# Quantising the fp4 stage's weights during the fourth rotary layer's feed-forward, and two tile copies taken ahead of the magnitudes

## The reference

```python
def fp4_quant_dequant(x):               # along the last dimension
    xb = x.reshape(shape[:-1] + (shape[-1] // 16, 16))
    scale = jnp.maximum(jnp.max(jnp.abs(xb), axis=-1, keepdims=True) / 6.0, 1e-12)
    xn = xb / scale
    idx = jnp.searchsorted(_MID, jnp.abs(xn))     # midpoints of 0 .5 1 1.5 2 3 4 6
    return (_GRID[idx] * jnp.sign(xn) * scale).reshape(shape)
def fp4_linear(x, w):
    return jnp.einsum('bsk,nk->bsn', fp4_quant_dequant(x), fp4_quant_dequant(w))
h = _silu(fp4_linear(x, w_gate)) * fp4_linear(x, w_up)      # w_gate, w_up: (352, 128)
return fp4_linear(h, w_down)                                # w_down: (128, 352)
```

## Time and profile before

| | us |
|---|---|
| median of 3 runs (6010.93 to 6014.99) | 6013.17 |
| profiled execution, its own time | 6008.89 |
| its span, first to last instruction | 6007.2 |
| fp4 stage within the span, first instruction 5394.99 to its last, ending 5698.75 | 304 |
| fourth layer's feed-forward alone on TensorE, about 4422 to 4549 | 127 |

### The profile page before, as it was taken

One profiled execution on the slowest core, in us unless ns is written; L12 is line 12 of the kernel. 1 busy time (PEld: TensorE's weight loads), 2 busy tenths in 40 slices (PEclk: granted clock), 3 DMA queues, 4 the chain that ended last, 5 costly groups with the idle time before them and its releaser, 6 DMA issues. The chain is left out here.

```text
span 6007.2 us, 119421 instructions
## 1 busy us (share of the span) xinstructions
PE 5516.8 (92%) x37438; PEld 3426.2 (57%) x37453; DVE 4177.6 (70%) x9588; ACT 2809.3 (47%) x4608; POOL 2256.1 (38%) x3170
## 2 busy tenths in 40 slices
PE   7997999999999899999999999999997879886687
PEld 5664444444444477657775677567754456644564
DVE  6785666666666688658874788478846866578764
ACT  4554222222222355545555555555555655534354
POOL 6662000000001466436653666356623532153212
PEclk9998999999999899999999999999998999898899
DMA  4333333333333555325542555055510000000002
GB/s 134 107 105 103 97 96 95 98 97 96 97 97 100 142 159 156 87 79 158 156 127 59 141 159 158 27 150 157 157 33 5 0 7 0 1 4 0 2 0 64
DMA packets 526333, 527.07 MB, mean 88 GB/s; under 512 B 55698, under 2 KB 436705, under 8 KB 503780
## 3 DMA queue, kind: packets, MB, share of 16 engines
q1 hardware_dynamic: 517684, 517.90, 31.5%
q10 hardware_dynamic: 8320, 5.25, 0.4%
HBM read 337.88 MB, written 185.07 MB: 87 GB/s over the span
## 5 line engine op out<-in xcount | busy, mean ns | idle before, releaser
L1121 DVE TENSOR_REDUCE a_mx<-a_unit 128x2 f32<-128x512 f32 (+1 forms) x1536 | 1033.9, 688 | 309.1 <-PE a_unit L1412 303.6
L1261 ACT ACTIVATE a_prob<-a_slot 128x1536 f32<-128x1536 f32 x512 | 742.9, 1451 | 550.1 <-PE a_slot L1435 464.8
L2098 ACT ACTIVATE f_silu<-f_pG 128x512 f32<-128x512 f32 x528 | 314.7, 597 | 935.1 <-PE f_pG L2182 921.1
L1410 PE MATMUL a_unit<-a_sk,a_sq 96*128 96x128 bf16 (+1 forms) x4096 | 597.5, 249 | 42.4 <-DMA a_sk<-a_kscratch 26.7
L2033 DVE TENSOR_TENSOR f_gated<-f_spread,f_silu 128x512 f32<-128x512 f32 x512 | 362.9, 709 | 341.2 <-ACT f_silu L2098 296.6
L2150 PE MATMUL f_pO<-f_hidden,f_wd 128*128 128x512 f32 x1056 | 546.3, 599 | 14.1 <-DVE f_hidden L2035 13.5
L60 POOL TENSOR_SCALAR f_veps<-f_moments 128x4 f32<-128x4 f32 (+1 forms) x112 | 25.3, 226 | 1420.1 <-DVE f_moments L1909 1020.4
L2182 PE MATMUL f_pG<-f_xnT,f_wg 128*128 128x512 f32 x1056 | 541.6, 594 | 0.0
L2186 PE MATMUL f_pU<-f_xnT,f_wu 128*128 128x512 f32 x1056 | 540.7, 594 | 0.0
L1412 PE MATMUL a_unit<-a_maskq,identb 128*128 128x256 bf16 (+1 forms) x1536 | 481.7, 314 | 2.1 <-issue 2.1
L1063 POOL TENSOR_SCALAR_AFFINE_SELECT a_prob<-a_prob 128x512 f32<-128x512 f32 x384 | 244.5, 637 | 519.4 <-ACT a_prob L1261 506.1
(11 more groups left out here) (473 smaller groups left out, 12165.1 us busy)
## 6 DMA issues: line engine op xcount, KB each, us to landing
f_spread<-f_scratch SPq DMA_DIRECT2D x1024, 128.0 KB, 2.9
a_sq<-a_qscratch SPq DMA_DIRECT2D x128, 768.0 KB, 5.6
a_sk<-a_kscratch SPq DMA_DIRECT2D x160, 384.0 KB, 6.6
a_qscratch<-a_parts SPq DMA_DIRECT2D x288, 192.0 KB, 2.2
a_qscratch<-a_parts SPq DMA_DIRECT2D x288, 128.0 KB, 2.2
a_kscratch<-a_parts SPq DMA_DIRECT2D x160, 192.0 KB, 2.2
a_kscratch<-a_parts SPq DMA_DIRECT2D x160, 128.0 KB, 2.2
a_qscratch<-a_parts SPq DMA_DIRECT2D x288, 64.0 KB, 1.8
```

Source lines behind the costliest of these rows:

```text
L1121: v.tensor_reduce(dst, src, op=ALU.max, axis=AX.X, negate=True).then_inc(red_done, 1)
L1261: act.activation(prob[gr % 2][:, :], slot[:, :], ACT.Exp, scale=SCALE).then_inc(exp_done, 1)
L1410: pe.matmul(bank[:, at * wide:(at + 1) * wide], q, sk[b][0:KM, gr * GH + h, 0:wide], start=(at == 0), stop=False)
L2098: act.activation(silu[c % 2][:, :], pG[c % 2][:, :], ACT.Silu).then_inc(silu_done, 1)
```

## The change

1. A class `Fp4Weights` takes over what `weights()` did. It owns the turned weights and seven semaphores for the whole program. In the fourth rotary layer's feed-forward, SyncE loads the weights and GpSimd blanks the unused rows once the last attention output is added; VectorE scales at s = 4 and 5 and rounds at s = 7 and 8; ScalarE takes the magnitudes at s = 6 and copies turned tiles at s = 9, 10 and 11, behind the second gelu; TensorE turns them at s = 9, 10 and 11, behind `widen(s, 0)`. The work lies in tiles of the attention. The same code leaves the fp4 stage.
2. In the fp4 stage's `step`, ScalarE copies turned tiles 0 and 1 ahead of the magnitudes of the gated rows.
3. The feed-forward's output tile `oT` is the attention's `ctxp`; two unused functions and two small unused tiles go.

```diff
+    def on_vector(self, v, chain, s):
+        if s == 4:
+            v.wait_ge(self.w_in, 80)
+            v.wait_ge(self.blank, 2)
+            self.scale(v, chain, self.raw, self.nsc, self.y)
+        if s == 5:
+            self.scale(v, chain, self.rawd, self.nscd, self.yd)
+            v.sem_inc(self.scaled, 1)
+        if s == 7:
+            v.wait_ge(self.magnitudes, 1)
+            self.round_to(v, chain, self.y, self.mag, self.nsc, self.done)
+        if s == 8:
+            self.round_to(v, chain, self.yd, self.magd, self.nscd, self.magd)
+            v.sem_inc(self.rounded, 1)
+    def on_scalar(self, act, s):
+        if s == 6:
+            act.wait_ge(self.scaled, 1)
+            act.activation(self.mag, self.y, ACT.Abs, scale=self.TWO_BITS)
+            act.activation(self.magd, self.yd, ACT.Abs, scale=self.TWO_BITS).then_inc(self.magnitudes, 1)
+        if s in (9, 10):
+            act.wait_ge(self.turned, s - 8)
+            at = (s - 9) * self.I
+            act.activation(self.wgu[:, at:at + self.I], self.bank[:, 0:self.I], ACT.Copy).then_inc(self.taken, 1)
...
+    def on_tensor(self, pe, s, ident):
+        if s in (9, 10):
+            pe.wait_ge(self.rounded, 1)
+            if s == 10:
+                pe.wait_ge(self.taken, 1)
+            for j, (lo, cnt) in enumerate(self.CUTS):
+                at = (3 * (s - 9) + j) * D
+                ins = pe.transpose(self.bank[:, lo:lo + cnt], self.done[0:cnt, at:at + D], ident[0:cnt, 0:cnt])
+            ins.then_inc(self.turned, 1)
...
@@ rotary_layers, SyncE and GpSimd, behind the last main_steps
+                sp.wait_ge(op_taken, SEQS)
+                q.load(sp)
...
+                g.wait_ge(op_taken, SEQS)
+                q.fill(g)
                 feed(False)
@@ VectorE, end of step s of feed
                         feed_stats(s)
+                        if not following:
+                            v.drain()
+                            q.on_vector(v, chain, s)
@@ fp4_feed_forward, VectorE
-                    if isinstance(n, int) and n == -3:
-                        weights()
@@ fp4_feed_forward, ScalarE
                     gate(1)
+                    if is_block(n - 1):
+                        turned_hidden(n - 1, 0)
+                        turned_hidden(n - 1, 1)
                     if is_block(n):
                         act.wait_ge(yh_done, n + 1)
                         act.activation(absh[:, :], yh[b][:, :], ACT.Abs, scale=TWO_BITS).then_inc(ah_done, 1)
-                    if is_block(n - 1):
-                        turned_hidden(n - 1, 0)
                     if is_block(n + 2):
                         act.wait_ge(yx_done, n + 3)
                         act.activation(absx[:, :], yx[:, :], ACT.Abs, scale=TWO_BITS).then_inc(ax_done, 1)
                     if is_block(n - 1):
-                        turned_hidden(n - 1, 1)
                         turned_hidden(n - 1, 2)
```

More of the change, by code:

```diff
@@ L111, in later @@
     return not isinstance(n, int) or n >= least
[L114 to L154, removed]
 KPART = [0, 1, 2, 0, 1, 0]
@@ L962, in rotary_layers @@
         mrow_in = [k.sem(f"mrow_in{b}") for b in range(4)]
+        q = core["fp4"]
+        q.work(o.rest[:, :, :].rearrange("p c t -> p (c t)"), o.f32s[:, :, :].rearrange("p c t -> p (c t)"), prob[0], prob[1], cT, ring[1])
         (w_in, fstats_done, frstd_done, fxn_done, ft_pe, fxnT_done, h_pe, gelu_done, o_pe, o_done, r_pe, r_taken,
@@ L1327, in feed @@
                         gelu(s + 1, 1)
+                        if not following:
+                            q.on_scalar(act, s)
                         if following and s in EARLY and EARLY[s] > -5:
@@ L1564, in feed @@
                                 o.turn_rows(pe, EARLY[s])
+                            if c == 0 and not following:
+                                q.on_tensor(pe, s, ident)
                             if c == 2:
@@ L2785, in fp4_feed_forward @@
         with nc.Block() as block:
-            @block.sync
-            def _(sp):
-                for c, name in ((0, "wg"), (3, "wu")):
-                    sp.dma_start(raw[:, c:c + 2, :], w[name][0:2 * P, :].rearrange("(c p) d -> p c d", p=P)
-                                 ).then_inc(w_in, 16)
-                    sp.dma_start(raw[0:I - 2 * P, c + 2, :], w[name][2 * P:I, :]).then_inc(w_in, 16)
-                sp.dma_start(rawd[:, :], w["wd"]).then_inc(w_in, 16)
             @block.gpsimd
@@ L2924, in _ @@
             def _(act):
-                def weights():
-                    act.wait_ge(wy_done, 1)
-                    act.activation(absh[:, 0:WGU], yh[0][:, 0:WGU], ACT.Abs, scale=TWO_BITS)
-                    act.activation(absx[:, 0:I], yx[:, 0:I], ACT.Abs, scale=TWO_BITS).then_inc(wa_done, 1)
-                    act.wait_ge(wt_pe, 1)
-                    for c in range(2):
-                        act.activation(wgu[:, c * I:(c + 1) * I], pG[c][:, 0:I], ACT.Copy)
-                    for c, (lo, cnt) in enumerate(CUTS):
-                        ins = act.activation(wd[0:cnt, c, :], pH[0:cnt, c * P:(c + 1) * P], ACT.Copy)
-                    ins.then_inc(wt_done, 1)
                 def step(i, j):
@@ L2988, in _ @@
                 ident = core["ident"]
-                pe.wait_ge(wq_done, 1)
-                for c in range(2):
-                    for j, (lo, cnt) in enumerate(CUTS):
-                        pe.transpose(pG[c][:, lo:lo + cnt], wdone[0:cnt, 3 * c + j, :], ident[0:cnt, 0:cnt])
-                for j, (lo, cnt) in enumerate(CUTS):
-                    ins = pe.transpose(pH[0:cnt, j * P:(j + 1) * P], wdoned[:, lo:lo + cnt], ident)
-                ins.then_inc(wt_pe, 1)
-                pe.wait_ge(wt_done, 1)
                 def step(i, j):
@@ L3649, in load_core @@
     core["ident"], core["identb"] = pool("ident", [P, P])[:, :], pool("identb", [P, P], BF16)[:, :]
[L3650 removed]
+    core["fp4"] = Fp4Weights(nc, pool, part_of(a, "q2_"))
     core["arriving"] = Arriving(nc, core, a)
```

85 lines of the change are left out of this document (62 added, 23 removed).

## The result

| | before | after |
|---|---|---|
| median, us (runs on one chip) | 6012.05 (4: 6010.64 to 6014.99) | 5971.4 (4: 5967.29 to 5980.0) |
| ratio | | 0.9928, 95% interval 0.9916 to 0.994 |
| profiled execution, its span | 6008.89, 6007.2 | 5974.55, 5972.8 |
| mean granted clock | 0.966 | 0.97 |

The change takes 40.6 us off the medians and 34.4 off the spans. Forecast were 23.25 us, and a time between 5983 and 6001: the direction was right, the size was not. The spans are accounted for here; the 6 us that the medians add are taken up further down.

What follows compares the result with a forecast made beforehand. VectorE has the most work in the fp4 stage, stalling 22.0 us on ScalarE's silu; TensorE bounds the rotary feed-forward. Terms -10.45, -0.3, +1.1, -10.2, +3, -2.1, -5.0, +0.7 sum to -23.25 us: 6013.2 to 5989.9, range 5983 to 6001.

Steps and rivals of the forecast that it cites:

- The opening: Start of the fp4 stage: without the weights VectorE takes block 0's rows 10.45 us earlier, at least 10, at most 11.
- The rotary feed-forward: Fourth rotary layer's feed-forward: the moved weight work adds 1.1 us, as TensorE is the bound; 1.0 to 4.
- The rival that saw it come out: Rotary stage: TensorE held at s = 9 to 11 by a late rounding, 3 to 6 us more, 5995; chance 0.07.
- The magnitudes: Fp4 loop, ScalarE: magnitudes of the gated rows start 1.0 us later, with 0.6 us in hand behind them.
- The rival of 6018 us: Fp4 loop: magnitudes come late, VectorE stalls 2.5 us in each block, about 6018 us in all; chance 0.06.
- The reserve for the clock (+3 us): Fp4 loop: 3 us for ten blocks together in case TensorE runs at the lower clock; ends none and 10 us.
- The rule weighed in the forecast: TensorE's array is throttled by default and activity releases it; after the moved gap 1.2 GHz, some 8 us less gain.
- The five stalls (-10.2 us): Fp4 loop: five blocks' fourth product waits 2.22 to 2.26 us for silu; copying tiles first leaves 0.2 of each.
- Block 15's product: Near the fp4 loop's end: the fourth product comes at 5672.7 instead of 5677.72, -5.0 us, or -3.7 with lower clock.
- The two blocks before it: Fp4 loop, two blocks before block 15's: 2.1 us of VectorE's stalls go in the same way, -2.1.
- The last block: End of the fp4 stage: slow last turns against GpSimd's earlier product, +0.7 us, between -2 and +1.
- The stages behind (0): Two untouched stages after the fp4 stage: the sum had no term for them, so a change of 0.

Runs made afterwards that it cites:

- e3: The changed kernel run once more, nothing altered, for a second trace and more times: 5988.88 us (5 runs), ratio 0.9943 against the kernel before.

## Why the prediction was wrong, point by point

The spans gained 34.4 us where 23.25 were forecast. Of the 11.2 us between, the stages behind are 5.7, the fifteen intervals 4.3, the last block 1.5 and two small terms 0.4; the opening takes 0.7 back. So two steps failed: a term that the sum did not have, and the price of the loop.

**The opening** was right: 10.47 us to block 0's maximum against 10.45. Of it 0.7 us was lost again before the first gated rows, which leaves 9.7, a little under the 10 that I gave as the least.

**The rotary feed-forward** was right: 1.07 us longer, 1.1 forecast, with 7.9 us of VectorE's work behind a TensorE that has hardly an idle moment. The rival that saw it come out did not occur. That the table's first row also comes near, with +0.8, is luck: this feed-forward began 1.1 us earlier, and the stage just ahead of the Fp4 stage took 1.3 us longer, which the change does not explain.

**The magnitudes** did not come 1 us late. In the block shown they start at the same distance from the block's first maximum as before, 4.70 us, and ScalarE still waited 1.11 us for the rows when it turned to them. The silus and copies ahead of them had moved forward instead. The rival of 6018 us had no ground.

**The reserve for the clock (+3 us)** was mis-sized, by 1.6 us, though its mechanism was there. These are all the stretches at the lower level between 5463 and 5651 us in the changed kernel, where the loop runs steadily (columns as above):

```profile
5489.88:5493.29 3.41, 3.41 (x12) 2.44 (x11) 3.19 (x5) 1.26 (x5) 2.15 (x3) 0.50 0.00 0
5520.60:5527.43 6.83, 6.23 (x17) 4.37 (x18) 6.35 (x10) 2.07 (x6) 2.93 (x6) 0.50 0.00 0
5544.49:5547.90 3.41, 3.41 (x7) 1.92 (x8) 3.00 (x6) 0.46 (x1) 1.98 (x2) 0.50 0.00 0
5568.39:5575.21 6.82, 5.76 (x16) 4.14 (x17) 6.51 (x12) 2.07 (x6) 3.07 (x5) 0.50 0.00 0
5602.52:5605.93 3.41, 3.41 (x13) 2.60 (x12) 3.19 (x5) 1.01 (x3) 1.62 (x2) 0.50 0.00 0
5633.24:5636.65 3.41, 3.06 (x11) 2.65 (x12) 3.26 (x4) 1.10 (x5) 0.00 (x0) 0.50 0.00 0
```

The two long ones cover the third and fourth gate-and-up, and just these two blocks have a stall behind it, 0.68 and 0.51 us, and took 16.67 and 16.38 us in place of 15.8 to 15.9. That is 1.4 us for the loop. The second trace of the changed kernel (e3) has one long stretch there, and one such block, 16.65 us. The kernel before had such a stretch in every block of this part, a long one in each of the five stalled blocks and a short one in each block between:

```profile
5534.76:5541.59 6.83, 6.11 (x22) 4.96 (x23) 6.04 (x7) 2.22 (x8) 3.19 (x4) 0.50 0.00 0
5551.83:5555.24 3.41, 3.05 (x15) 2.75 (x15) 3.19 (x10) 1.61 (x5) 2.85 (x5) 0.50 0.00 0
```

So the stall that the prediction costed had the clock in it, and the new order shortened or removed most of these stretches.

The rule weighed in the forecast (the Trainium skill, TensorE: Matmul & The Clock Gate, The HAM clock gate) would have made the gain some 8 us smaller. The cold stretches agree with it in part: four of the six, both long ones among them, begin within 1.1 us of the end of a TensorE gap of 3.2 to 3.3 us, the other two are behind no gap above 2 us. The size doesn't agree, since VectorE's pace left room for it in most blocks.

**The five stalls (-10.2 us)** were costed nearly right as stalls, and short as a loop. Three of the stalled blocks went from 18.2 to 15.9 us, 2.3 less and not 2.04 (the earliest to 16.14, and one to the 16.67 above), and each block between them, which I took as it was, gave 0.17 us too (15.94 to 15.77). VectorE's own pace, 14.40 us busy and 1.37 of issue, bounds both sorts, and a block without a stall had stood only 0.17 us above it. Over the five and the four between, with the 1.4 us of the clock set aside, this is about 1.7 us more than the term had. With VectorE's pace as the new floor, thirteen blocks at 15.77 to 15.89 us give intervals of 231.1 to 232.7 us, with the first and the last as measured; with 1.4 us for the clock that is the 233.1 measured. Counted from the kernel before, that floor gives a gain of 18 to 19.5 us with the forecast's 5.0 for block 15; the forecast's own terms without the reserve give 17.3. What was "late next" I had asked within the block, not over the loop.

**Block 15's product**: its interval fell by 5.6 us in the first pair of traces, 5.0 forecast. **The two blocks before it** gave 2.2, 2.1 forecast. **The last block** was 0.8 us shorter rather than 0.7 longer, inside the range down to -2 that I gave. Three of the four last turns were slow, as foreseen (0.85 to 0.90 us each, the fourth 0.49), but GpSimd's earlier start outweighed it.

**The stages behind (0)**, 5.7 us, was the other failed step, and the largest: no part of the working had a place for it, and no reason was given for nothing. Of it 2.8 us is the attention's steady rhythm, shown by the drains to go by the place of VectorE's code. The rest stays open. It is 0.8 us from that stage's first statistics to its first maximum (10.53 to 9.71 us), 1.1 in the first interval and 1.0 in the last stage. Each of these stretches varies over the thirteen traces by as much or more with no pattern that goes by the edit: the first has one of two values, the last stage takes 141.5 to 145.6 us. So a part of the 5.7 us may be luck of the pair of traces; the second trace of the changed kernel had 4.3 of it.

**The medians**: I took the offset of 4.3 us between trace and median as the only spread. Between chips and runs the unchanged code ahead moves by up to 14 us. Forecast and result would have differed by 9 us on the second chip (32.2 us gained) and by 17 on the first. The range was too narrow for that as well.

## What to carry to other kernels

When an edit removes stalls from a software-pipelined loop, cost it twice: stall by stall, and as the old period less the busiest engine's work plus its issue time. The second is the floor for all blocks, the stalled and the others. Here the two gave 17.3 and 18 to 19.5 us, and 18.6 were measured; what pulled the forecast down to 14.3 was a reserve that no row had sized. Before giving work to an engine that looks idle, look at which of the other's instructions it will lie beside, since GpSimd and VectorE held each other here and the relief became a loss. And adding or removing instructions on VectorE shifts every later loop of it in the code, which can move an untouched stage, here by 2.8 us; two drains of 0.02 us in front of such a loop shortened it here, though the whole kernel's time did not show it.

## What the runs showed of the hardware that was not expected

- VectorE's first row after the jump to the head of a loop had 0.28, 0.39 or 0.49 us of issue for the same code at different places, and the period of the loop was 9.03, 9.14 or 9.24 us with it: 2.8 us over the stage between the first and the last.
- A VectorE rounding of 128 x 1408 elements took 2.48 instead of 1.63 us beside a GpSimd product of 128 x 512, and a GpSimd product of 128 x 4 took 1.54 instead of 0.56 us beside that rounding.
- One loop ran in two rhythms with nearly the same rate: 15.94 and 18.17 us in turn, or 16.7 to 17.2 throughout, both 252 us for fifteen blocks. In the first, the long blocks were those whose stretch at the lower clock lasted twice as long.
